# A mixture-of-experts stage: gate and up projected with the weights stationary, from a two-deep ring that ScalarE fills

## The reference

```
logits = x @ gate_w.T                     # 16 experts
p = sigmoid(logits); p = p / sum(p)
w, idx = top_k(p, 2); w = w / sum(w)
gate, up = split(x @ gate_up_proj[e])     # 256 -> 2 x 128
inter = silu(gate) * up
y = inter @ down_proj[e]                  # 128 -> 256
out[t] = sum over the two chosen experts of w * y
```

## Time and profile before

| | us |
|---|---|
| median of 3 runs | 527.75 |
| lowest, highest | 527.48, 530.24 |
| the profiled execution, its own time | 526.13 |
| its span, first to last instruction | 524.3 |
| TensorE busy | 489.1 (93%) |
| VectorE busy | 378.5 (72%) |
| ScalarE busy | 350.3 (67%) |
| GpSimd busy | 316.4 (60%) |
| mean granted TensorE clock | 0.982 |

### The profile page before, as it was taken

One profiled execution on the slowest core, in us unless ns is written; L12 is line 12 of the kernel. 1 busy time (PEld: TensorE's weight loads), 2 busy tenths in 40 slices (PEclk: granted clock), 3 DMA queues, 4 the chain that ended last, 5 costly groups with the idle time before them and its releaser, 6 DMA issues.

```text
span 524.3 us, 10836 instructions
## 1 busy us (share of the span) xinstructions
PE 489.1 (93%) x3625; PEld 431.1 (82%) x3648; DVE 378.5 (72%) x833; ACT 350.3 (67%) x791; POOL 316.4 (60%) x319
## 2 busy tenths in 40 slices
PE   8899999999999997799975999999999999999994
PEld 7678888888888786588854888999999999999884
DVE  4798888878874266655555899879757985588556
ACT  5758888877877755344432788768766876676663
POOL 5759898889886136345560688776554564465330
PEclk9999999999999999799996999999999999999999
DMA  7939999950000492345575000000000000000001
GB/s 260 397 101 385 316 316 322 329 181 1 1 2 1 151 376 83 103 132 163 163 261 191 2 0 1 1 1 3 1 1 0 1 2 2 1 0 1 2 22 60
DMA packets 17761, 56.84 MB, mean 108 GB/s; under 512 B 2628, under 2 KB 12362, under 8 KB 15914
## 3 DMA queue, kind: packets, MB, share of 16 engines
q1 hardware_dynamic: 14960, 49.81, 28.0%
q0 software_dynamic: 2752, 6.40, 3.7%
HBM read 49.19 MB, written 28.45 MB: 148 GB/s over the span
## 4 chain that ended last, share of the span: by engine, by line
PE 60%; POOL 9%; DVE 8%; issue 8%; ACT 7%; DMA 6%; SPq 1%; POOLq 0%; ACTq 0%; DVEq 0%
PE bank L450 10%; PE bank L452 9%; PE bank L451 9%; PE bank L1007 5%; PE bank L515 4%; DMA wvo_raw<-in_wvo 4%; POOL qT L2030 3%; ACT probs L1138 3%; PE bank L1024 2%; PE bank L751 2%; PE bank L736 2%; PE bank L738 2%; PE bank L737 2%; POOL probs L2038 2%; PE bank L627 2%
## 5 line engine op out<-in xcount | busy, mean ns | idle before, releaser
L1138 ACT ACTIVATE probs<-bank,neg_max,q_scale 128x256 f32<-128x256 f32 (+1 forms) x128 | 63.8, 509 | 22.0 <-DVE neg_max L1822 22.0
L2080 POOL TENSOR_TENSOR exps<-exps,tables 128x256 f32<-128x256 f32 x32 | 25.7, 802 | 70.8 <-ACT exps L1253 70.7
L2038 POOL TENSOR_TENSOR probs<-probs,inv_sum 128x512 f32<-128x512 f32 x64 | 51.7, 829 | 21.8 <-DVE inv_sum L1830 21.7
L1253 ACT ACTIVATE exps<-bank 128x768 f32<-128x768 f32 x32 | 25.9, 809 | 37.8 <-PE bank L718 37.7
L2176 POOL DMA_INDIRECT y_rows<-y_slot,dest x31 | 29.8, 961 | 30.3 <-issue 19.0
L1635 DVE TENSOR_TENSOR q_lo<-q_sum,q_hi 128x512 fp32r<-128x512 f32 x32 | 29.0, 906 | 26.0 <-ACT q_hi L1207 25.7
L2067 POOL TENSOR_TENSOR swapped<-swapped,tables 128x512 f32<-128x512 f32 x32 | 43.2, 1352 | 5.9 <-ACT swapped L1174 5.7
L1808 DVE TENSOR_TENSOR swapped<-bank,tables 32x512 f32<-32x512 f32 x64 | 44.4, 693 | 1.4
L2030 POOL TENSOR_TENSOR qT<-qT,swapped 128x512 f32<-128x512 f32 x32 | 41.0, 1283 | 6.2 <-DVE swapped L1808 6.2
L450 PE MATMUL bank<-x,wq_hi 128*128 128x256 f32 x128 | 38.5, 301 | 0.1
L450 PE MATMUL bank<-wo_hi,c_hi 128*128 128x256 f32 x128 | 37.5, 293 | 0.0
(11 more groups left out here) (291 smaller groups left out, 1827.5 us busy)
## 6 DMA issues: line engine op xcount, KB each, us to landing
slots<-in_c_unused SPq DMA_DIRECT2D x20, 1036.0 KB, 35.8
gu_all<-in_gate_up SPq DMA_DIRECT2D x4, 1024.0 KB, 8.5
xg<-slots SPq DMA_DIRECT2D x31, 129.5 KB
wvo_raw<-in_wvo SPq DMA_DIRECT2D x1, 2560.0 KB, 19.0
dn_all<-in_down SPq DMA_DIRECT2D x1, 2048.0 KB, 7.7
wq_full<-in_Wq SPq DMA_DIRECT2D x1, 2048.0 KB
wo_raw<-in_Wo SPq DMA_DIRECT2D x1, 2048.0 KB
wqk_raw<-in_wqk SPq DMA_DIRECT2D x1, 1536.0 KB, 9.9
```

Of the source, the lines that this page charges most:

```text
L1138: ins = act.activation(probs[:, par, h, c0:c1], bank[:, 2 * par + h, c0:c1], ACT.Exp, bias=neg_max[:, par, i:i + 1], scale=q_scale[:, b, t ...
L2038: ins = pool.tensor_tensor(some, some, inv, ALU.mult)
```

## The change

- `up` swaps its operands. The stationary operand is now a 128x128 piece of the block's gate or up weights, and `xgT` streams, 128 columns: four matmuls (gate and up, two halves of the contraction each) in place of two. The result has the hidden units on the partitions.
- So the transpose of the product (`turn_act`) and its copy (`copy_act`) go. VectorE's multiplication writes `actT` directly. Down runs one step behind up, not two, and so does `copy_y`. The loops have `STEPS + 1` steps.
- The stationary operand is no longer read from `gu_all` at an address from a register. A new function on ScalarE, `take_weights(k)`, loads block k's expert into a register of ScalarE and copies its 128x512 floats from `gu_all` to `gu_block`, a ring of two (`GU`) that lies in `q_sum`, which is free in this stage. `up` waits for it on a new semaphore, `gu_copied`. Blocks 0 and 1 are taken ahead of the first xgT copy; block k+2 behind the silu of block k.
- TensorE still loads each block's expert, for down.

```diff
+GU = 2
...
-    gated, act_tok = (swapped[:, i, 0:2 * FF].rearrange("p (i n) -> p i n", i=2) for i in range(2))
+    gu_block = q_sum[:].rearrange("p g (c f) -> p g c f", c=KD)
+    gated = swapped[:, 0, 0:2 * P].rearrange("p (i n) -> p i n", i=2)
...
                 mm = pe.transpose(bank[:, turned(k), c * P:c * P + P], xg[:, k % XG, c * P:c * P + P], ident[:])
             mm.then_inc(mo["xgT_done"], 1)
-        def up(k, experts):
+        def up(k):
             pe.wait_ge(mo["xgT_copied"], k + 1)
+            pe.wait_ge(mo["gu_copied"], k + 1)
             if k >= 2:
                 pe.wait_ge(mo["act_ready"], k - 1)
-            for c in range(KD):
-                for i, e in enumerate(experts):
-                    rows = slice(ROWS * i, ROWS * i + ROWS)
-                    mm = pe.matmul(bank[rows, up_bank(k), 0:2 * FF], xgT[:, k % 2, c, rows],
-                                   gu_all[:, bass.ds(e, 1), c, :].rearrange("p e f -> p (e f)"),
-                                   start=c == 0, stop=c == KD - 1, skip_group_check=True)
+            for i in range(PER_STEP):
+                rows = slice(ROWS * i, ROWS * i + ROWS)
+                for half in range(2):
+                    dst = bank[:, up_bank(k), half * P + ROWS * i:half * P + ROWS * i + ROWS]
+                    for c in range(KD):
+                        mm = pe.matmul(dst, gu_block[:, k % GU, c, half * FF:half * FF + FF], xgT[:, k % 2, c, rows], start=c == 0, stop=c == KD - 1,
+                                       skip_group_check=True)
             mm.then_inc(mo["up_done"], 1)
-        def turn_act(k):
+        def down(k, experts):
             pe.wait_ge(mo["act_ready"], k + 1)
-            if k >= 2:
-                pe.wait_ge(mo["actT_copied"], k - 1)
-            pe.transpose(bank[:, actT_bank(k), 0:P], act_tok[:, k % 2, :], ident[:]).then_inc(mo["actT_done"], 1)
-
-        def down(k, experts):
-            pe.wait_ge(mo["actT_copied"], k + 1)
             if k >= 2:
                 pe.wait_ge(mo["y_copied"], k - 1)
             for i, e in enumerate(experts):
...
             pe.wait_ge(x_or_expert_in[j], 32)
         turn_block(0)
         experts_of = {}
-        for i in range(STEPS + 2):
+        for i in range(STEPS + 1):
             if i < STEPS:
                 experts_of[i] = [pe.value_load(block_expert[0:1, m:m + 1], min_val=0, max_val=E - 1)
                                  for m in range(PER_STEP * i, PER_STEP * i + PER_STEP)]
             if i + 1 < STEPS:
                 turn_block(i + 1)
             if i < STEPS:
-                up(i, experts_of[i])
-            if 1 <= i <= STEPS:
-                turn_act(i - 1)
-            if i >= 2:
-                down(i - 2, experts_of.pop(i - 2))
+                up(i)
+            if i >= 1:
+                down(i - 1, experts_of.pop(i - 1))
         pe.wait_ge(mo["y_copied"], STEPS)
         pe.wait_ge(y_back[0], 16)
...
             act.activation(xgT[:, k % 2, :, :], bank[:, turned(k), 0:D].rearrange("p (c n) -> p c n", c=KD),
                            ACT.Copy).then_inc(mo["xgT_copied"], 1)
+        def take_weights(k):
+            e = act.value_load(block_expert[0:1, k:k + 1], min_val=0, max_val=E - 1)
+            if k >= GU:
+                act.wait_ge(mo["up_done"], k - GU + 1)
+            act.activation(gu_block[:, k % GU, :, :], gu_all[:, bass.ds(e, 1), :, :].rearrange("p e c f -> p (e c) f"),
+                           ACT.Copy).then_inc(mo["gu_copied"], 1)
+
         def silu(k):
             act.wait_ge(mo["up_done"], k + 1)
             if k >= 2:
                 act.wait_ge(mo["act_ready"], k - 1)
-            act.activation(gated[:, k % 2, :], bank[:, up_bank(k), 0:FF], ACT.Silu).then_inc(mo["silu_done"], 1)
+            act.activation(gated[:, k % 2, :], bank[:, up_bank(k), 0:P], ACT.Silu).then_inc(mo["silu_done"], 1)
         act.wait_ge(ld["wq1_in"], 16)
         act.wait_ge(ln["y_done"], NT)
         for i in range(PAIRS):
             act.activation(chunk(wq_hi, i), chunk(wq_full, i), ACT.Copy).then_inc(kv["w_hi"], 1)
+        act.wait_ge(mo["table_steps"], 4)
+        for j in range(4):
+            act.wait_ge(x_or_expert_in[j], 32)
+        take_weights(0)
+        take_weights(1)
         copy_block(0)
         for k in range(STEPS):
             if k + 1 < STEPS:
                 copy_block(k + 1)
             silu(k)
+            if k + 2 < STEPS:
+                take_weights(k + 2)
         load_table(act, 2 * B + 8, ACT.Sqrt)
         act_layer1(act)
...
         def gate_block(k):
             dve.wait_ge(mo["silu_done"], k + 1)
             if k >= 2:
-                dve.wait_ge(mo["actT_done"], k - 1)
-            dve.tensor_tensor(act_tok[:, k % 2, :], gated[:, k % 2, :], bank[:, up_bank(k), FF:2 * FF],
+                dve.wait_ge(mo["down_done"], k - 1)
+            dve.tensor_tensor(actT[:, k % 2, :], gated[:, k % 2, :], bank[:, up_bank(k), P:2 * P],
                               ALU.mult).then_inc(mo["act_ready"], 1)
-
-        def copy_act(k):
-            dve.wait_ge(mo["actT_done"], k + 1)
-            if k >= 2:
-                dve.wait_ge(mo["down_done"], k - 1)
-            dve.tensor_copy(actT[:, k % 2, :], bank[:, actT_bank(k), 0:P]).then_inc(mo["actT_copied"], 1)
         def copy_y(k):
             dve.wait_ge(mo["down_done"], k + 1)
...
                                      in1=xg[:, k % XG, D + 2:D + 3], op0=ALU.not_equal,
                                      op1=ALU.add).then_inc(mo["dest_ready"], 1)
-        for i in range(STEPS + 2):
-            if 1 <= i <= STEPS:
-                copy_act(i - 1)
+        for i in range(STEPS + 1):
             if i < STEPS:
                 gate_block(i)
                 find_rows(i)
-            if i >= 2:
-                copy_y(i - 2)
+            if i >= 1:
+                copy_y(i - 1)
         dve_layer1(dve, counted, n_step)
```

More of the change, by code:

```diff
@@ L307, in build @@
               "table_sums table_steps "
-              "xgT_done xgT_copied up_done silu_done act_ready actT_done actT_copied down_done y_copied dest_ready")
+              "xgT_done xgT_copied gu_copied up_done silu_done act_ready down_done y_copied dest_ready")
     kv = sems("kv1", "kv_hi kv_lo w_hi w_lo k_done swap_done cos_done sin_done k_summed "
@@ L386, in up_bank @@
         return 2 + k % 2
-    def actT_bank(k):
-        return 4 + k % 2
     def down_bank(k):
```

## The result

The changed kernel takes 536.10 us in the median (533.14 to 538.31, four runs), the kernel before on the same chip 528.02 (527.48 to 530.24). The ratio is 1.0152, with a 95% interval of 1.0114 to 1.019: 8.1 us slower, where I had forecast 3.4 faster, and outside my range. The execution profiled took 536.72 us, its span is 534.7.

A forecast was written before the change was run, and what follows sets the result against it. TensorE's streaming through 31 blocks and a serial tail were taken to bound the expert stage. Gains of 2.2 us (steady part, less the start's 0.04) and 1.2 (tail) made 3.4: median 527.75 to 524.3, range 522.5 to 528.5.

The forecast's parts named there:

- TensorE's terms: Expert block on TensorE: transposes 0.22, gate and up 0.90 (eight instructions, 0.112 each), down 0.43; 1.55 us, before 1.63.
- rival 4: Gate and up on TensorE: no floor beyond streaming at 128 columns, block 1.51 us, total 523.2; chance 0.09.
- rival 3: Gate and up on TensorE: weights' floor 0.122 per instruction, block 1.63 us, only the tail gained, 526.5; chance 0.08.
- ScalarE's chain: ScalarE per block, from silu's start: load 0.73, weight copy 0.52, xgT copy about 0.30; next silu could start at 1.55.
- Rivals 1: ScalarE's or TensorE's register loads don't hide: block up to 1.60 us, gain 2.0, total 525.8; chance 0.22.
- rival 2: ScalarE becomes the bound, its load starting only after silu: block 1.83 us, loss 4.5, total 532.2; chance 0.11.
- Start: First to third product: 2.83 us against 2.79 before, as TensorE's expert load still lies open; 0.04 lost.
- Steady part: Third product to last: 28 steps at 1.547 us in place of 1.627; 2.2 us gained.
- (a): Weights loop, product through silu, ScalarE's load and copies to product k+2: 2.89 us for two blocks, 3.09 available.
- (b): TensorE's own expert load, queued behind down, which waits for the multiplication: 2.81 us of 3.09 for two blocks.
- (c): VectorE's multiplication must end before down: 0.79 us behind the product's streaming, while down comes 1.55 behind it.
- Tail: Last product to last scatter: 4.19 us against 5.43 before, capped by GpSimd's scatter spacing of 1.27; 1.2 us gained.

The follow-up runs named there:

- a_noassert: The changed kernel with only the range checks of loaded registers left out of the loads on TensorE, ScalarE and SyncE; 524.31 us, ratio 0.9939.
- a_lean_static: The changed kernel with seven implied waits per block left out and experts fixed by block number, so no register loads on TensorE and ScalarE; 523.05 us, ratio 0.9879.
- a_fixed_expert: The changed kernel, but ScalarE copies a fixed expert's weights (block number modulo 16) and loads no register; 536.27 us, ratio 1.0169.
- a_lean_sync: The changed kernel with seven implied waits per block left out and seven satisfied waits added on SyncE's queue behind each fetch; 536.24 us, ratio 1.0133.
- a_best_sync: a_lean_noassert with four satisfied waits added to SyncE's queue behind each fetch; 523.59 us, ratio 0.9929.
- a_lean_noassert: The changed kernel with seven implied waits per block and the range checks of loaded registers (TensorE, ScalarE, SyncE) left out; 523.80 us, ratio 0.9916.
- b_lean: The kernel before with the waits implied by the engines' order and the range checks of loaded registers left out; 527.68 us, ratio 0.9986.

## Why the prediction was wrong, point by point

- *TensorE's terms.* Right. 0.89, 0.43 and 0.22 in the chain for 0.90, 0.43 and 0.22; starts 0.112 apart; steps of 1.55. Pure streaming (rival 4) and 0.122 (rival 3) are out. So is the 107 ns that the rule of the Trainium skill gives for 128 columns ("TensorE: Matmul & The Clock Gate", section "LDWEIGHTS (loading the stationary operand)"): eight would be 0.86, the row has 0.89.
- *ScalarE's chain.* Right in sum, and with more room than I gave it: the weight copy starts 0.64 to 0.71 behind silu in nearly all blocks of a_noassert, not 0.73, and the load takes 282 ns in the median. The floor of about 600 ns that the Trainium skill gives for a register load ("DMA: Bandwidth & Descriptors", section "Latency and other measured facts") doesn't hold for it. Rivals 1 and 2 are out: in a_noassert TensorE waits 0.4 us in all for an xgT copy, once. That 536.1 lies near rival 2's 532.2 is chance; ScalarE is idle 2.31 at the place where that rival had it busy.
- *Start.* 2.83 was forecast. In the changed kernel's variants at full clock it is 2.76 (a_lean_static) to 3.10 (a_fixed_expert). In others it is 4.3 to 4.5, and that is the clock (below). The profiled execution of the kernel after is one of them: 4.29, with a granted clock of 0.50 in 224 to 226, behind a stretch (220 to 222) in which TensorE was busy for 0.07 of 2.00 us. Those 1.5 us stood in no term of mine.
- *Steady part.* 43.3 forecast for the 28 steps, 43.20 in a_noassert, 51.25 after. This is the step that failed. The sum moved each instruction and each wait to its new place and took for granted that a semaphore arrives as promptly as before, at once after the matmul. That rested on a row of the kernel before and wasn't priced when the stage became denser: 7.95 us. I named loops (a), (b) and (c) with their slack down to 0.20 in two blocks, but no rival for something that all queues share, though SyncE's queue and its load and check stood in the rows and I called it free, since it fetches six blocks ahead. It had slack, but a_noassert against the kernel after says that what it runs isn't without effect.
- *Tail.* 1.2 gained was the forecast (4.2 from the last product to the last scatter, 5.43 before). The kernel after has 5.76, 0.3 lost: the silus of its last two blocks come 2.04 and 0.69 behind their products. This term failed by the same step. It is 3.69 to 3.76 in a_lean_static, a_lean_sync, a_best_sync and a_lean_noassert: the scatter of the last block but one starts 2.43 behind the last product in a_lean_static and not 2.92, because there it follows its copy by 0.28 and not by the 0.76 that I took over from the earlier trace rows. Others have 3.9 to 5.01. The 5.01 are a_noassert's, which so keeps 0.4 of the 1.2; there VectorE's copy of y waits for the landing of an older scatter, a wait that I had put at nothing. That row, then the timeline of a_lean_static:

```profile
270.25 0.89 DVE L2007 COPY y_slot<-bank 128x256 f32<-128x256 f32 x2 [0.64 <-DMA y_rows<-y_slot,dest]
```

```profile
267.35 1.05 PE L1005 MATMUL bank<-xgT,q_sum 128*128 128x128 f32 x8
...
269.08 0.42 DVE L1992 COPY y_slot<-bank 128x256 f32<-128x256 f32 x1
...
269.78 0.96 POOL L2159 DMA_INDIRECT y_rows<-y_slot,dest  x1 [0.37 <-DVE y_slot L1992]
...
271.04 0.96 POOL L2159 DMA_INDIRECT y_rows<-y_slot,dest  x1 [0.31 <-issue]
```

- *Sum.* 3.4 forecast for the change; without SyncE's check it brings 0.61% (0.31 to 0.91), that is 3.2 us, and with the implied waits gone too 0.84% (0.54 to 1.14), 4.4 us. As it stands it loses 8.1. In the profiled execution, forecast at 522.7 and measured at 536.72, all but 0.3 of the 14.0 us between are 7.95 of the steady part, 1.5 of the start, 1.6 of the tail and 2.7 from before the stage.
- *What would show it.* I had listed idle time of TensorE once a block, ended by a copy or its own queue. It came about every third block instead, and the row to look at was ScalarE's: an idle time ended by a product that had long been issued.

## What to carry to other kernels

When a change packs a stage tighter, the durations of its instructions carry over, the promptness of its semaphores may not: give that a rival of its own, and after the run compare the distance from a product's last instruction to its consumer, block by block, before looking for a slow engine. Register loads with range checks on a queue that "only issues DMAs" belong to the budget of the stage; here, leaving the checks out, which takes two instructions per block off SyncE and moves the others to where the register is used, turned a loss of 8.1 us into a gain of about 3. Look for rows that are shorter than the same work elsewhere (68 ns for a load of 270): they were there before the change. And a change should be judged again once such a side effect is gone, since the mechanism that it was made for was sound.

## What I had not expected of the hardware

- Semaphore updates of TensorE that arrive up to 2.3 us late and in a bunch, while its matmuls go on starting 0.112 apart; and, in the kernel before too, rows of SyncE that are far too short or too long (a load of 68 ns, a check of 252 in place of 18).
- Waits that are already satisfied, four pairs a block on VectorE and on ScalarE, cost the kernel before 3.5 us (b_records), and four on SyncE with four on VectorE cost a_lean_noassert nothing that can be measured (523.89 against 523.80).
- The first blocks run at either clock. In a_noassert TensorE's granted clock is at its lower level, 1.2 GHz, for most of 220 to 224 (0.60 and 0.54 in the two stretches), and the first two products take 1.6 to 1.7 each; in a_best_sync, behind the same idle matmuls, it stays at 2.4 GHz. That is 1.3 us between two executions, and the kernel before has it too in some (2.79 from first to third product in the one profiled, 3.69 in b_lean, with 0.57 in 222 to 224). Windows of a_noassert, then of a_best_sync (columns as at the top, the clock ahead of the last two):

```profile
220.00:222.00 2.00, 2.00 (x12) 1.96 (x12) 0.00 (x0) 0.47 (x3) 0.00 (x0) 0.60 0.65 179
222.00:224.00 2.00, 2.00 (x11) 2.00 (x10) 0.42 (x2) 1.13 (x3) 0.00 (x0) 0.54 0.03 8
```

```profile
220.00:222.00 2.00, 1.83 (x15) 1.74 (x16) 0.00 (x0) 1.04 (x3) 0.00 (x0) 1.00 0.77 209
222.00:224.00 2.00, 1.95 (x16) 1.66 (x15) 1.01 (x5) 1.65 (x5) 0.00 (x0) 1.00 0.01 4
```
